# Two edits to a one-core transformer-block kernel: the first weight matrix is split before the first input is normalised, and the end of the last stage is rearranged

## The chip, the core and the metric

The kernel runs on one core of one Trainium2 chip, as one program. The metric is the device time of a run in microseconds, from start to end; the median of several runs is compared. A core has five engines that run their own instruction streams and wait for each other by semaphores: TensorE (PE, matmuls; its weight loads are shown as PEld), VectorE (DVE), ScalarE (ACT), GpSimd (POOL) and SyncE (SP), which here only issues the DMAs.

## The reference, cut to what matters

```python
xn = layernorm(x)                                   # x: 8 x 1024 rows of 512, no gain or offset
h  = performer_attn(xn, wq, wk, wv, wo, omega)      # random-feature attention, 16 heads
y  = layernorm(xn + h, ln1_g, ln1_b)
h2 = gelu(y @ w1 + b1) @ w2 + b2                    # 512 -> 2048 -> 512
a  = layernorm(y + h2, ln2_g, ln2_b)
r  = sigmoid(mix_r(xn) @ W_r.T) * (square(relu(mix_k(xn) @ W_k.T)) @ W_v.T)
return x + a + r
```

All is float32. Each product is made of three fast products: a matrix is split into a rounded part "hi" and a rest "lo", and hi*hi, hi*lo and lo*hi are summed (`TERMS`, `product`).

## The kernel before, in words

Three passes run one after the other: `keys_pass` (normalise x, queries, keys, values, the sums over keys), `attend_pass` (attention output and gated block) and `feed_forward_pass`. Each works on 32 groups of `GT` = 256 rows (tokens), a group being `TG` = 2 token tiles of 128 partitions. Each engine has its own program; the order of the jobs in it is written out by hand (`HEAD` and the `..._BODY` lists in the first pass, `BODY` in the last). An engine does its jobs strictly in that order, and a job begins with its semaphore waits.

**Start of the first pass.** SP issues the loads of omega, of the first group of x (`keys_xin`) and of six half matrices of weights (`keys_e` holds those of wk and wq, `keys_z_sum` those of wv, 512 KB each). For the first group: DVE makes the statistics (`stats`, L222 to L228), POOL inverts the deviation (`norm.invert`, L233 `rstd` and L235 `shift`), ACT normalises (`norm`, L475, `keys_xn`), PE transposes in two halves (`turn_x`, L608), ACT and DVE split each half into `xT_hi` (L482) and `xT_lo` (L546), and POOL adds the two for a copy to memory (`whole`, L442, `keys_xT_whole`). A weight matrix is split in two pieces: ACT rounds each into hi (L183), DVE takes the rest into lo (L190). PE's first product (job `k`) waits for the split xT and for both pieces of wk.

**The last pass.** Per group g, PE makes eight blocks of the hidden layer (`w1`, into `ffn_hidden`), each followed three steps later by its part of the second product (`w2`, into `ffn_result`): w1 0, 1, 2, w2 0, w1 3, w2 1, w1 4, w2 2, w1 5, w2 3, ... w1 7, the transposes of the next group's y (`turn`, L1514), w2 5, 6, 7. Between them ACT takes the gelu (L1451) and the rounded part (L1460), and DVE the rest `ffn_hT_lo` (L1484); w2 n waits for `hT_lo` n. In DVE's order the job `base` stands between `hT_lo` 2 and `hT_lo` 3: it waits for the DMA of `ffn_r_in` and makes `x_in` = 0.5 r + x (L1489). The end of a group: DVE adds `ffn_result` and `yb` into `ffn_s` (L1496) and makes the statistics; POOL inverts; ACT normalises `ffn_s` (L1464, two tiles); POOL multiplies by the gain (L1418), adds the offset (L1421) and adds `x_in` (L1425), each over both tiles at once; SP stores `x_in`. Then POOL makes `yb` of the next group (L1413). SP, after `yb`, loads the next y, waits for the store of `x_in` to have landed, and loads the next `x_in` and `r_in` (L1393, L1394). So `base` of a group waits for POOL's end of the group before. Groups 1 to 30 run in a hardware loop; groups 0 and 31 are written out.

Of the kernel before, what the change touches and what calls it, by code (L numbers as in the profile page):

```python
# [6 lines left out]
ALU = mybir.AluOpType  # L7
# [3 lines left out]
P = 128  # L11
D = 512
# [8 lines left out]
TG = 2  # L21
# [221 lines left out]
def keys_pass(nc, x, wq, wk, wv, omega, xn_d, xT_d, u_d, kv_d, n_batches, groups_per_batch):  # L243
# [5 lines left out]
    G = n_batches * groups_per_batch  # L249
# [5 lines left out]
    with ctx:  # L255
# [31 lines left out]
        norm = Norm(mem, ctx, "n0", EPS0)  # L287
# [55 lines left out]
        def rows(j):  # L343
# [15 lines left out]
        POOL_BODY = [("whole", 0, 1), ("z", 0, 0), ("stats", 0, 2), ("z", 1, 0), ("z", 2, 0), ("z", 3, 0),  # L359
                     ("z", 4, 0), ("z", 5, 0), ("z", 6, 0), ("z", 7, 0)]  # L360
        SP_BODY = [("x", 0, 2), ("whole", 0, 1), ("sums", 0, -1), ("q", 1, 1), ("norm", 0, 2)]
        HEAD = [("x", 0, 0), ("stats", 0, 0), ("norm", 0, 0), ("turn_x", 0, 0), ("turn_x", 1, 0), ("x", 0, 1),
                ("whole", 0, 0), ("weights", 0, 0), ("weights", 1, 0), ("k", 0, 0), ("weights", 2, 0), ("k", 1, 0),
                ("stats", 0, 1), ("sq", 0, 0), ("q", 0, 0), ("norm", 0, 1), ("sq", 1, 0), ("q", 1, 0),
                ("turn_k", 0, 0), ("turn_k", 1, 0), ("v", 0, 0), ("v_out", 0, 0), ("v", 1, 0), ("v_out", 1, 0),
                ("turn_x", 0, 1), ("turn_x", 1, 1)]
# [913 lines left out]
def feed_forward_pass(nc, x, w1, b1, w2, b2, ln2_g, ln2_b, y_d, r_d, out, n_groups):  # L1280

    G = n_groups
# [6 lines left out]
    with ctx:  # L1289
# [13 lines left out]
        s = sb("s", [P, TG, D])  # L1303
# [65 lines left out]
        def _(sp):  # L1369
            sp.dma_start(y[:, :, :], y_g[0]).then_inc(y_loaded, 16)  # L1370

            def do(job, n, g):
# [10 lines left out]
                if job == "base":  # L1383
# [8 lines left out]
                        sp.wait_ge(w_split, len(pieces))  # L1392
                    sp.dma_start(x_in[:, :, :], x_g[g]).then_inc(xr_loaded, 16)  # L1393
                    sp.dma_start(r_in[:, :, :], r_g[g]).then_inc(xr_loaded, 16)  # L1394
                if job == "end":
                    sp.wait_ge(done, g + 1)
                    sp.dma_start(out_g[g], x_in[:, :, :]).then_inc(stored, 16)

            run(sp, do)
            sp.wait_ge(y_loaded, 16 * (G + 1))  # L1400
            sp.wait_ge(stored, 16 * G)

        @block.gpsimd
        def _(pool):
            make_identity(pool, ident, ident_made)
            norm.init(pool)
            pool.wait_ge(consts_loaded, 16 * 4)

            def do(job, n, g):
                if job == "base":  # L1410
                    pool.wait_ge(y_loaded, 16 * g + 16)
                    wait(pool, sum_ready, TG * g)
                    pool.tensor_tensor(yb[:, :, :], y[:, :, :], bias2[:, :].unsqueeze(1).broadcast_to([P, TG, D]),  # L1413
                                       ALU.add).then_inc(yb_ready, 1)
                if job == "end":
                    norm.invert(pool, g)
                    pool.wait_ge(normed, TG * g + TG)
                    pool.tensor_tensor(s[:, :, :], s[:, :, :], gain[:, :].unsqueeze(1).broadcast_to([P, TG, D]),  # L1418
                                       ALU.mult).then_inc(gained, 1)
                    pool.wait_ge(gained, g + 1)  # L1420
                    pool.tensor_tensor(s[:, :, :], s[:, :, :], offset[:, :].unsqueeze(1).broadcast_to([P, TG, D]),  # L1421
                                       ALU.add).then_inc(offsets, 1)
                    pool.wait_ge(offsets, g + 1)
                    pool.wait_ge(base_ready, g + 1)
                    pool.tensor_tensor(x_in[:, :, :], s[:, :, :], x_in[:, :, :], ALU.add).then_inc(done, 1)  # L1425

            run(pool, do)
# [42 lines left out]
        def _(dve):  # L1470
            def do(job, n, g):
# [19 lines left out]
                if job == "end":  # L1491
                    for t in range(TG):
                        dve.wait_ge(result[t].full, g + 1)
                        dve.wait_ge(yb_ready, g + 1)
                        wait(dve, done, g)
                        dve.tensor_tensor(s[:, t, :], result[t].t[:, :], yb[:, t, :], ALU.add).then_inc(sum_ready, 1)  # L1496
                    dve.wait_ge(sum_ready, TG * g + TG)
                    wait(dve, norm.ready, g)
                    norm.reduce(dve, g, [s[:, t, :] for t in range(TG)])

            run(dve, do)

# [95 lines left out]
```

## Time and profile before

| | |
|---|---|
| median of 3 runs | 3691.76 us (3691.68 to 3693.3) |
| the profiled execution | 3692.05 us, its span 3690.2 us |
| PE, PEld, DVE, ACT, POOL busy | 96%, 84%, 56%, 50%, 38% |
| start of the last pass's steady part (first transposes) | 2228.48 us |

The span is what the profile covers; 1.85 us of the time lie outside it. Busy shares are means over the three passes and hide short waits, of which the start and the end of the program are made.

### The profile page before, as it was taken

How to read it: one execution, taken by the hardware profiler on the slowest of the kernel's cores; microseconds unless marked ns; L12 is line 12 of the kernel's file. 1: busy time of each engine (PE TensorE's matmuls, PEld its weight loads, DVE VectorE, ACT ScalarE, POOL GpSimd, SP SyncE). 2: the span in 40 equal slices, each digit the busy share in tenths (PEclk: the TensorE clock that was granted, in tenths of full speed). 3: DMA queues.
4: the chain of work that ended last, by engine and by line, in shares of the span. 5: the costliest groups of instructions: out<-in, count | busy, mean ns of one | idle time of the engine just before them, and what ended most of it. 6: DMA issues, size and time to landing. Idle time of an engine off the chain costs nothing. (4 is left out here: it accounts for less than half of the span.)

```text
span 3690.2 us, 71667 instructions
## 1 busy us (share of the span) xinstructions
PE 3544.2 (96%) x27762; PEld 3105.4 (84%) x27762; DVE 2070.7 (56%) x3304; ACT 1839.5 (50%) x3976; POOL 1394.2 (38%) x957
## 2 busy tenths in 40 slices
PE   7999999999699999999999949999999999999998
PEld 6888888887588888888888849988889989888887
DVE  5877777777567777777777633333333333333332
ACT  5777777777456656565665633333333323333332
POOL 2554545454244545454454412222222222222222
PEclk9999999999799999999999979999999999999999
DMA  2222222221223232232323241111111111111111
GB/s 104 87 78 70 90 78 73 73 88 54 95 81 102 82 97 91 88 97 88 102 84 98 83 129 68 46 44 43 45 44 46 45 38 46 44 43 45 45 45 46
DMA packets 151680, 262.70 MB, mean 71 GB/s; under 512 B 23184, under 2 KB 44176, under 8 KB 151440
## 3 DMA queue, kind: packets, MB, share of 16 engines
q1 hardware_dynamic: 151440, 259.46, 20.9%
q8 instruction: 155, 2.54, 0.3%
q14 instruction: 85, 0.70, 0.1%
HBM read 155.48 MB, written 103.94 MB: 70 GB/s over the span
## 5 line engine op out<-in xcount | busy, mean ns | idle before, releaser
L1484 DVE TENSOR_TENSOR ffn_hT_lo<-ffn_hid,ffn_hT_hi 128x512 fp32r<-128x512 f32 x256 | 334.3, 1334 | 489.4 <-ACT ffn_hT_hi L1460 489.4
L97 PE MATMUL ffn_hidden<-ffn_yT_hi,ffn_wa_hi 128*128 128x256 f32 x2048 | 573.3, 280 | 11.8 <-DVE ffn_yT_lo L1480 11.8
L97 PE MATMUL ffn_hidden<-ffn_yT_hi,ffn_wa_lo 128*128 128x256 f32 x2048 | 573.3, 280 | 0.0
L97 PE MATMUL ffn_hidden<-ffn_yT_lo,ffn_wa_hi 128*128 128x256 f32 x2048 | 572.3, 279 | 0.0
L1451 ACT ACTIVATE ffn_hid<-ffn_hidden,ffn_bias 128x256 f32<-128x256 f32 x512 | 213.2, 467 | 669.6 <-PE ffn_hidden L97 650.8
L233 POOL TENSOR_TENSOR ffn_n_rstd<-ffn_n_base,ffn_n_power 128x2 f32<-128x2 f32 x32 | 22.4, 700 | 1073.7 <-DVE ffn_n_negmean L228 1073.7
L97 PE MATMUL ffn_result<-ffn_wb_hi,ffn_hT_hi 128*128 128x512 f32 x1024 | 412.2, 403 | 2.6 <-DVE ffn_hT_lo L1484 2.6
L97 PE MATMUL ffn_result<-ffn_wb_hi,ffn_hT_lo 128*128 128x512 f32 x1024 | 404.5, 395 | 0.0
L97 PE MATMUL ffn_result<-ffn_wb_lo,ffn_hT_hi 128*128 128x512 f32 x1024 | 404.2, 395 | 0.0
L97 PEld LDWEIGHTS ffn_hidden<-ffn_yT_hi,ffn_wa_hi 128*128 128x128 f32 x2048 | 384.5, 188 | 20.8 <-DVE ffn_yT_lo L1480 12.1
L97 PEld LDWEIGHTS ffn_hidden<-ffn_yT_lo,ffn_wa_hi 128*128 128x128 f32 x2048 | 385.0, 188 | 8.8
L97 PEld LDWEIGHTS ffn_hidden<-ffn_yT_hi,ffn_wa_lo 128*128 128x128 f32 x2048 | 385.2, 188 | 0.0
L457 POOL TENSOR_TENSOR keys_z_sum<-keys_z_sum,keys_e 128x512 f32<-128x512 f32 x192 | 265.2, 1402 | 307.3 <-ACT keys_e L512 307.3
L512 ACT ACTIVATE keys_e<-keys_feat,keys_below 128x128 f32<-128x128 f32 x1024 | 280.6, 420 | 22.8 <-DVE keys_below L569 22.7
L575 DVE SCALAR_TENSOR_TENSOR keys_pk_lo<-keys_e,keys_pk_hi 128x512 fp32r<-128x512 f32 x256 | 219.3, 887 | 25.7 <-ACT keys_pk_hi L519 25.5
L97 PEld LDWEIGHTS ffn_result<-ffn_wb_hi,ffn_hT_hi 128*128 128x128 f32 x1024 | 192.1, 188 | 48.4 <-DVE ffn_hT_lo L1484 10.2
L97 PEld LDWEIGHTS ffn_result<-ffn_wb_hi,ffn_hT_lo 128*128 128x128 f32 x1024 | 192.2, 188 | 46.9
L1107 DVE TENSOR_REDUCE attend_top<-attend_feat 128x4 f32<-128x512 f32 x256 | 159.0, 684 | 125.3 <-PE attend_feat L1200 125.3
L1126 DVE SCALAR_TENSOR_TENSOR attend_pT_lo<-attend_feat,attend_pT_hi 128x512 fp32r<-128x512 f32 x256 | 163.3, 683 | 116.7 <-ACT attend_pT_hi L988 116.3
L97 PEld LDWEIGHTS ffn_result<-ffn_wb_lo,ffn_hT_hi 128*128 128x128 f32 x1024 | 192.4, 188 | 38.0
L565 DVE TENSOR_REDUCE keys_top<-keys_feat 128x4 f32<-128x512 f32 x256 | 159.0, 684 | 107.7 <-PE keys_feat L652 107.7
L1464 ACT ACTIVATE ffn_s<-ffn_s,ffn_n_shift,ffn_n_rstd 128x512 f32<-128x512 f32 x64 | 48.7, 809 | 338.7 <-POOL ffn_n_shift L235 338.7
(238 smaller groups left out, 9876.8 us busy)
## 6 DMA issues: line engine op xcount, KB each, us to landing
attend_uq<-u_d SPq DMA_DIRECT2D x33, 512.0 KB, 4.6
ffn_y_in<-y_d SPq DMA_DIRECT2D x33, 512.0 KB, 3.6
keys_xin<-in_L_attn_x_dram SPq DMA_DIRECT2D x32, 512.0 KB, 5.3
xn_d<-keys_xn SPq DMA_DIRECT2D x32, 512.0 KB, 4.2
xT_d<-keys_xT_whole SPq DMA_DIRECT2D x32, 512.0 KB, 2.6
u_d<-keys_uq SPq DMA_DIRECT2D x32, 512.0 KB, 2.8
attend_xTf<-xT_d SPq DMA_DIRECT2D x32, 512.0 KB, 5.1
r_d<-attend_gate SPq DMA_DIRECT2D x32, 512.0 KB, 3.2
```

What stands on the lines that cost most here:

```text
L97: last = pe.matmul(out, stationary[a], moving[b], start=start and n == 0, stop=stop and n == len(TERMS) - 1)
L233: pool.tensor_tensor(self.rstd[:, :], self.base[:, :], self.power[:, :], ALU.pow).then_inc(self.root, 1)
L457: pool.tensor_tensor((z_all if last_of_batch else z_sum)[:, c, :], z_sum[:, c, :], e[t][:, c, :], ALU.add).then_inc(z_added[t], 1)
L512: last = act.activation(e[t][:, c, j * M:(j + 1) * M], feat[j].t[:, c * M:(c + 1) * M], ACT.Exp, bias=below[:, t, h:h + 1])
L565: dve.tensor_reduce(top[:, n, :, j:j + 1], feat[j].t[:, :].rearrange("p (c m) -> p c m", c=NC), AX.X, ALU.max).then_inc(top_ready, 1)
L575: dve.scalar_tensor_tensor(out=pk[t].lo[:, c, :], in0=e[t][:, c, :], scalar=FLOOR, in1=f32(pk[t].hi[:, c, :]), op0=ALU.add, op1=ALU.subtract)\
L1107: dve.tensor_reduce(top[:, n, :, j:j + 1], feat[j].t[:, :].rearrange("p (c m) -> p c m", c=NC), AX.X, ALU.max).then_inc(feat[j].free, 1)
L1126: dve.scalar_tensor_tensor(out=pT[j].lo[:, :], in0=feat[j].t[:, :], scalar=FLOOR, in1=f32(pT[j].hi[:, :]), op0=ALU.add, op1=ALU.subtract)\
L1451: last = act.activation(hid[n % 2][:, a, :], bank.t[:, a * GT:(a + 1) * GT], ACT.Gelu, bias=bias1[:, 2 * n + a:2 * n + a + 1])
L1464: act.activation(s[:, t, :], s[:, t, :], ACT.Identity, bias=norm.shift[:, t:t + 1], scale=norm.rstd[:, t:t + 1]).then_inc(normed, 1)
L1484: dve.tensor_tensor(hT[n % HB].lo[:, :, :], hid[n % 2][:, :, :], f32(hT[n % HB].hi[:, :, :]), ALU.subtract).then_inc(h_ready[n % HB], 1)
```

## The change

Three edits. In `HEAD`, the job `("weights", 0, 0)` moves from behind the first group's normalisation and transposes to a place between its statistics and its normalisation. In the last pass, POOL adds the offset to `x_in` right after `base`, before the inversion, in every group, and no longer to `s` behind the gain. In the last group alone, POOL's multiplication and final addition go to DVE, by token tiles of 512 columns, and SP stores each tile by itself.

```diff
-        HEAD = [("x", 0, 0), ("stats", 0, 0), ("norm", 0, 0), ("turn_x", 0, 0), ("turn_x", 1, 0), ("x", 0, 1),
-                ("whole", 0, 0), ("weights", 0, 0), ("weights", 1, 0), ("k", 0, 0), ("weights", 2, 0), ("k", 1, 0),
+        HEAD = [("x", 0, 0), ("stats", 0, 0), ("weights", 0, 0), ("norm", 0, 0), ("turn_x", 0, 0), ("turn_x", 1, 0),
+                ("x", 0, 1), ("whole", 0, 0), ("weights", 1, 0), ("k", 0, 0), ("weights", 2, 0), ("k", 1, 0),
...
# SP
-                if job == "end":
+                if job == "end" and isinstance(g, int) and g == G - 1:
+                    for t in range(TG):
+                        sp.wait_ge(done, g + 1 + t)
+                        sp.dma_start(out_g[g][:, t, :], x_in[:, t, :]).then_inc(stored, 16)
+                elif job == "end":
                     sp.wait_ge(done, g + 1)
                     sp.dma_start(out_g[g], x_in[:, :, :]).then_inc(stored, 16)
...
# POOL
                 if job == "end":
+                    pool.wait_ge(base_ready, g + 1)
+                    pool.tensor_tensor(x_in[:, :, :], x_in[:, :, :], offset[:, :].unsqueeze(1).broadcast_to([P, TG, D]),
+                                       ALU.add).then_inc(offsets, 1)
                     norm.invert(pool, g)
+                if job == "end" and not (isinstance(g, int) and g == G - 1):
                     pool.wait_ge(normed, TG * g + TG)
                     pool.tensor_tensor(s[:, :, :], s[:, :, :], gain[:, :].unsqueeze(1).broadcast_to([P, TG, D]),
                                        ALU.mult).then_inc(gained, 1)
                     pool.wait_ge(gained, g + 1)
-                    pool.tensor_tensor(s[:, :, :], s[:, :, :], offset[:, :].unsqueeze(1).broadcast_to([P, TG, D]),
-                                       ALU.add).then_inc(offsets, 1)
                     pool.wait_ge(offsets, g + 1)
-                    pool.wait_ge(base_ready, g + 1)
                     pool.tensor_tensor(x_in[:, :, :], s[:, :, :], x_in[:, :, :], ALU.add).then_inc(done, 1)
...
# DVE
+                if job == "end" and isinstance(g, int) and g == G - 1:
+                    dve.wait_ge(offsets, G)
+                    for t in range(TG):
+                        dve.wait_ge(normed, TG * g + t + 1)
+                        dve.tensor_tensor(s[:, t, :], s[:, t, :], gain[:, :], ALU.mult).then_inc(gained, 1)
+                        dve.wait_ge(gained, g + 1 + t)
+                        dve.tensor_tensor(x_in[:, t, :], s[:, t, :], x_in[:, t, :], ALU.add).then_inc(done, 1)
```

What stands in a row on an engine, at the places the prediction speaks of. First VectorE at the start of the first pass (`keys_wk_lo` is the rest of the first weight matrix, `keys_xT_lo` that of the transposed first group); ScalarE's order changes alike, with `keys_wk_hi` now ahead of `keys_xn`:

```order
 L228 TENSOR_SCALAR keys_n_negmean<-keys_n_mv 128x2
+L190 TENSOR_TENSOR keys_wk_lo<-keys_e,keys_wk_hi 128x1024 x2
 L546 TENSOR_TENSOR keys_xT_lo<-keys_turn,keys_xT_hi 128x512 x2
-L190 TENSOR_TENSOR keys_wk_lo<-keys_e,keys_wk_hi 128x1024 x2
 L190 TENSOR_TENSOR keys_wq_lo<-keys_e,keys_wq_hi 128x1024 x2
```

The two instructions move from behind the split of xT to before it. Next GpSimd in the body of the last pass's loop:

```order
-L1413 TENSOR_TENSOR ffn_yb<-ffn_y_in,ffn_bias 128x1024
+L1417 TENSOR_TENSOR ffn_yb<-ffn_y_in,ffn_bias 128x1024
+L1420 REGISTER_ALU
+L1421 TENSOR_TENSOR ffn_x_in<-ffn_x_in,ffn_offset 128x1024
 L231 ISA
-L232 REGISTER_ALU
 L233 TENSOR_TENSOR ffn_n_rstd<-ffn_n_base,ffn_n_power 128x2
 L234 REGISTER_ALU
 L235 TENSOR_TENSOR ffn_n_shift<-ffn_n_negmean,ffn_n_rstd 128x2
-L1417 REGISTER_ALU
-L1418 TENSOR_TENSOR ffn_s<-ffn_s,ffn_gain 128x1024
-L1421 TENSOR_TENSOR ffn_s<-ffn_s,ffn_offset 128x1024
-L1425 TENSOR_TENSOR ffn_x_in<-ffn_s,ffn_x_in 128x1024
```

The addition of the offset goes from between gain and final addition to a place ahead of the inversion; gain and final addition follow the inversion as before, as L1426 and L1430. Last, the end of VectorE's program after the change:

```order
L1501 TENSOR_TENSOR ffn_s<-ffn_result,ffn_yb 128x512 x2
L222 BN_STATS ffn_n_stats<-ffn_s 128x6 x2
L225 BN_AGGR ffn_n_mv<-ffn_n_stats 128x2 x2
L227 TENSOR_SCALAR ffn_n_base<-ffn_n_mv 128x2
L228 TENSOR_SCALAR ffn_n_negmean<-ffn_n_mv 128x2
L1509 TENSOR_TENSOR ffn_s<-ffn_s,ffn_gain 128x512
L1511 TENSOR_TENSOR ffn_x_in<-ffn_s,ffn_x_in 128x512
L1509 TENSOR_TENSOR ffn_s<-ffn_s,ffn_gain 128x512
L1511 TENSOR_TENSOR ffn_x_in<-ffn_s,ffn_x_in 128x512
```

The last four rows are new; the two operations of 1024 columns that they replace have left GpSimd's program.

## Rows read from the trace of the kernel before

**Rows 1.** The page: the chain that ended last, by line

```profile
PE ffn_result L97 19%; PE ffn_hidden L97 18%; PE ffn_turn L1514 1%; DMA ffn_r_in<-r_d 1%; POOL ffn_s L1421 0%; POOL ffn_s L1418 0%; POOL ffn_yb L1413 0%; SPq L1376 0%; DMA ffn_s<-in_L_attn_w_dram 0%; ACT ffn_s L1464 0%; DVE ffn_s L1496 0%; POOL ffn_n_rstd L233 0%; DVE ffn_hT_lo L1484 0%; POOLq L1289 0%; SPq L1388 0%
```

**Rows 2.** Timeline of the first 22 us: start, duration, operation, [idle before, releaser]

```profile
9.32 0.20 POOL L235 TENSOR_TENSOR keys_n_shift<-keys_n_negmean,keys_n_rstd 128x2 f32<-128x2 f32 x1
9.55 1.52 ACT L475 ACTIVATE keys_xn<-keys_xin,keys_n_shift,keys_n_rstd 128x512 f32<-128x512 f32 x2 [4.87 <-POOL keys_n_shift L235]
...
15.41 1.99 ACT L183 ACTIVATE keys_wk_hi<-keys_e 128x1024 fp32r<-128x1024 f32 x2
15.55 0.69 DVE L546 TENSOR_TENSOR keys_xT_lo<-keys_turn,keys_xT_hi 128x512 fp32r<-128x512 f32 x1 [1.90 <-ACT keys_xT_hi L482]
16.32 2.35 POOL L442 TENSOR_TENSOR keys_xT_whole<-keys_xT_hi,keys_xT_lo 128x1024 f32<-128x1024 f32 x1 [6.81 <-DVE keys_xT_lo L546]
16.50 4.40 DVE L190 TENSOR_TENSOR keys_wk_lo<-keys_e,keys_wk_hi 128x1024 fp32r<-128x1024 f32 x2 [0.25 <-ACT keys_wk_hi L183]
...
20.95 0.80 PE L97 MATMUL keys_ring<-keys_wk_hi,keys_xT_hi 128*128 128x512 f32 x1 [6.06 <-DVE keys_wk_lo L190]
```

**Rows 3.** The instructions on `keys_wk_lo`: duration ns min/median/max, first and last start

```profile
L190 DVE TENSOR_TENSOR keys_wk_lo<-keys_e,keys_wk_hi x2: 1210/2238/3265, 16.5 to 19.7; 128x1024 fp32r<-128x1024 f32 x2
```

**Rows 4.** Loads of wk: issues, then landing after issue, first half and second half

```profile
3.08 0.98 SPq L161 DMA_DIRECT2D keys_e<-in_L_attn_wk_dram  x2
...
keys_e<-in_L_attn_wk_dram SPq DMA_DIRECT2D x1, 512.0 KB, 4.6
...
keys_e<-in_L_attn_wk_dram SPq DMA_DIRECT2D x1, 512.0 KB, 5.4
```

**Rows 5.** Stretches: length, busy (count) of PE, PEld, DVE, ACT, POOL, PEclk, DMA share, GB/s

```profile
20.90:25.80 4.90, 4.85 (x11) 3.84 (x12) 2.26 (x2) 0.00 (x0) 0.00 (x0) 1.00 0.00 0
25.80:34.30 8.50, 8.50 (x38) 6.99 (x37) 5.24 (x10) 5.21 (x8) 0.90 (x2) 1.00 0.00 0
```

**Rows 6.** Timeline of PE, last pass: transposes that open groups' periods, first, two neighbours, last

```profile
2228.48 0.38 PE L1514 MATMUL ffn_turn<-ffn_ident,ffn_y_in 128*128 128x128 f32 x2
...
3479.45 0.38 PE L1514 MATMUL ffn_turn<-ffn_ident,ffn_y_in 128*128 128x128 f32 x2
...
3525.57 0.38 PE L1514 MATMUL ffn_turn<-ffn_ident,ffn_y_in 128*128 128x128 f32 x2
...
3618.50 0.27 PE L1514 MATMUL ffn_turn<-ffn_ident,ffn_y_in 128*128 128x128 f32 x1
```

**Rows 7.** Waits in the last pass, 2200 to 3690 us: total, times, longest

```profile
PEld ffn_result L97 <- DVE ffn_hT_lo L1484: 10.2, 43, 1.7
```

**Rows 8.** Timeline of one group's end and the next group's `base`, by engine

```profile
3589.32 2.72 POOL L1421 TENSOR_TENSOR ffn_s<-ffn_s,ffn_offset 128x1024 f32<-128x1024 f32 x1
3594.82 2.85 POOL L1413 TENSOR_TENSOR ffn_yb<-ffn_y_in,ffn_bias 128x1024 f32<-128x1024 f32 x1
...
3605.26 1.23 DVE L1489 SCALAR_TENSOR_TENSOR ffn_x_in<-ffn_r_in,ffn_x_in 128x1024 f32<-128x1024 f32 x1 [9.85 <-DMA ffn_r_in<-r_d]
3606.40 1.28 DVE L1484 TENSOR_TENSOR ffn_hT_lo<-ffn_hid,ffn_hT_hi 128x512 fp32r<-128x512 f32 x2
...
3607.14 0.50 PE L97 MATMUL ffn_result<-ffn_wb_hi,ffn_hT_hi 128*128 128x512 f32 x1 [0.15 <-DVE ffn_hT_lo L1484]
```

**Rows 9.** Timeline of the last 20 us

```profile
3666.35 0.69 DVE L1484 TENSOR_TENSOR ffn_hT_lo<-ffn_hid,ffn_hT_hi 128x512 fp32r<-128x512 f32 x1 [4.93 <-ACT ffn_hT_hi L1460]
...
3676.91 1.52 ACT L1464 ACTIVATE ffn_s<-ffn_s,ffn_n_shift,ffn_n_rstd 128x512 f32<-128x512 f32 x2 [10.60 <-POOL ffn_n_shift L235]
3678.51 2.34 POOL L1418 TENSOR_TENSOR ffn_s<-ffn_s,ffn_gain 128x1024 f32<-128x1024 f32 x1 [1.63 <-ACT ffn_s L1464]
...
3685.70 0.39 SPq L1397 DMA_DIRECT2D out_dram<-ffn_x_in  x1
```

**Rows 10.** DMA from 3685 to 3691 us: busy tenths in 40 slices of 0.15 us, and landing

```profile
DMA  0000000000299999989800000000000001000000
...
out_dram<-ffn_x_in SPq DMA_DIRECT2D x1, 512.0 KB, 2.8
```

More of the change, by code:

```diff
@@ L1400, in _ @@
             sp.wait_ge(y_loaded, 16 * (G + 1))
-            sp.wait_ge(stored, 16 * G)
+            sp.wait_ge(stored, 16 * G + 16)
         @block.gpsimd
```

## The prediction

> **What bounds the kernel now.** The chain that ended last comes first [rows 1]: it lies almost wholly on TensorE, but a DMA of `ffn_r_in`, three GpSimd lines of the last pass and a few other waits stand in it. So a change off TensorE counts only where TensorE waits: at the start, at such a wait in the last pass, and at the end. The next views were read for these places.
>
> At the start the timeline shows TensorE's first product at 20.95 us, 0.05 after the second `keys_wk_lo` is done (16.50 + 4.40 = 20.90). The split of the input, its other condition, was complete at 15.55 + 0.69 = 16.24 [rows 2]. The first weight matrix is what is late there, by 4.66 us. It is late for two reasons: ScalarE rounds it only after the input's transposes, and its first rest took 3265 ns where the second took 1210 [rows 3], since GpSimd's `keys_xT_whole` ran from 16.32 to 18.67 [rows 2].
>
> In the last pass, the steps from transposes to transposes: 30 periods take 3618.50 - 2228.48 = 1390.0 us, 46.33 on average, where two neighbours are 3525.57 - 3479.45 = 46.12 apart, the least of the 30 [rows 6]. The surplus is 1390.0 - 30 x 46.12 = 6.4 us. Where it sits is seen in one period [rows 8]: `base` waits for `r_in` until 3605.26, `hT_lo` 3 stands behind it and ends at about 3606.40 + 0.65 = 3607.05, and TensorE starts w2 3 at 3607.14, after a wait of 0.15 and with a first matmul of 0.50. Waits for `hT_lo` come 43 times, 10.2 us in all, the longest 1.7 [rows 7]; part of them stand before w2 0, which waits behind ScalarE's end of the group, not behind `base`.
>
> At the end nothing runs beside the chain: ScalarE 1.52 us, three GpSimd operations from 3678.51, the store at 3685.70, and its landing after 2.8 us [rows 9, 10].
>
> **The change, part by part.** All sums are against the profiled execution, 3692.05 us (span 3690.2 and 1.85 outside it); the median of the runs is 0.29 lower.
>
> *First matrix ahead of the normalisation.* Eight instructions change place (two ACT, two DVE ahead of two `xn`, two `xT_hi`, two `xT_lo`); none is added and SP's queue keeps its order. The halves of wk land at 3.08 + 4.6 = 7.68 and about 3.57 + 5.4 = 8.97 [rows 4]. ScalarE takes about 1.04 each (1.99 for two [rows 2]), so it is done with both at about 10.0 and normalises then instead of at 9.55: 0.45 later. DVE's rests follow from about 8.75. Here something new can be late: `shift` on GpSimd at 9.32 reads two SBUF operands for 0.20 us, and would find the first rest, 1.21 us long [rows 3], under way. One such pair is seen [rows 2, 3]: the rest began behind `xT_whole` and lasted 18.67 - 16.50 + 1.1 = 3.27. If `shift` waits in the same way, until about 10.35, ScalarE starts at about 10.55, 1.0 later than now. I take 1.0; the other bound is 0.45. The split of the input is then complete at 17.24 and TensorE starts at 17.3, with both rests of wk done by about 12. Gain 3.65 us (4.2 by the other bound).
> Every product after it follows, if wq is ready: ScalarE rounds wq from about 16.4, GpSimd's `xT_whole` (2.35) holds DVE until 19.7, two rests of 1.21 end at about 22.1. TensorE asks for it 24 matmuls after 17.3. At the last pass's rate (46.12 us for 192 matmuls of 256 columns and 96 of 512, so 0.24 per 512) this is 23.1. So it is covered by 1 us even if TensorE is fast at once.
> TensorE's granted clock is 1.00 in both stretches, but 11 matmuls take 4.85 us after its 6 us of idleness, 0.44 each (the level of 1.2 GHz), and then 38 take 8.50, 0.22 each (2.4 GHz) [rows 5]. The slow stretch can come out shorter or longer behind a shorter pause: none at all would give 2.4 us more, all 24 matmuls of job `k` slow would cost 13 x 0.22 = 2.9. I take it as unchanged.
>
> The Trainium skill (SBUF — State Buffer, SBUF: two separate sides) says that a VectorE operation with two SBUF inputs and a GpSimd operation that reads SBUF exclude each other, the first to start keeping the ports for its whole length; by it `shift` waits and the sum is the 3.65 taken.
>
> *Offset on `x_in` after `base`, groups 0 to 30.* One operation of 1024 columns (2.72 [rows 8]) leaves the path from ScalarE's end to `done`, `yb`, the loads and `base`; it is not shortened but moved to a stretch in which GpSimd has nothing else to do. All four steps behind it (store, y load, `x_in`, `r_in`) start 2.72 earlier, so `hT_lo` 3 does too. The longest wait is 1.7 [rows 7], so all of the surplus goes: 6.4 us. What is moved lands right behind `base`, which ends at 3606.49 (old clock), while `hT_lo` 3 starts at 3606.40 [rows 8], before GpSimd can have its semaphore. So it runs first. `hT_lo` 4 is then held by up to 2.35, to 3607.68 + 2.35 - 2.72 = 3607.3, while TensorE asks for it only after w2 3 and w1 6, over 5 us after 3607. That cover gone, each us would cost 31. If instead `hT_lo` 3 is held, it ends at 3606.49 - 2.72 + 2.35 + 0.65 = 3606.8 instead of 3607.05, and nearly nothing is gained: bounds 6.4 and 0. I take 6.4, since the start at 3606.40 is the nearer row.
> In the last group the same operation lies a period after 3606.49, before 3656, 20 us before it is needed.
>
> *The last end on DVE, by tiles.* Removed: three GpSimd operations, 3678.51 to 3685.7. Added: four DVE operations of 512 columns with two SBUF inputs, like `hT_lo`, 0.69 [rows 9]. The first tile is normalised at 3676.91 + 0.76 = 3677.67, the second at 3678.43, before DVE asks for it. 3677.70 + 4 x 0.69 + 3 x 0.03 for the waits = 3680.55. The last store is issued at 3680.57 instead of 3685.70: 5.1 us (4.8 if each wait takes 0.1 more). It moves half as much. The data of the 512 KB flow in ten slices of 0.15 us, 1.5 us, from 0.8 after the issue [rows 10]; the first tile's store, issued 1.4 earlier, is out of the way. So half the data saves 0.75 (bounds 0 and 0.75; I take 0.75, since nothing else is in flight). Together 5.85.
>
> The Trainium skill (DMA: Bandwidth & Descriptors, Anatomy of one DMA — SWDGE (gpsimd) path) gives each DMA a fixed 2.0 us plus bytes at 436 GB/s, which speaks against cutting a store: by it the last half takes 2.6 us, 0.2 less than the whole here, and the sum falls by 0.55. It is written for DMAs of the GpSimd queue; the 512 KB would take 3.2 by it, and the row has 2.8, so the row is followed.
>
> Sum: 3.65 + 6.4 + 5.85 = 15.9; 3692.05 - 15.9 - 0.29 = 3675.9, rounded to 3676.
>
> **The rivals.** What a measurement of this kernel can tell from no change is 0.2%, 7.4 us.
> *GpSimd's offset holds `hT_lo` 3.* For it: the pairs of [rows 2, 3] show how fully one engine holds the other. Against it: the order of starts. Loop 0 to 3 instead of 6.4: 3679 to 3682.5.
> *The start gives little.* `shift` waits longer than thought, or the slow stretch of TensorE grows by its bound of 2.9: start 0.7, in all 3679.
> *It does not do what it says.* `r_in` lands no earlier, because the store or a load takes the 2.72 back, and the start gives nothing: only the end's 5.85 is left, 3686, no change that can be told. The loads follow GpSimd closely in the trace, which speaks against it.
> *Slower.* The place is DVE behind `base`. If `hT_lo` 3 is held by GpSimd for 2.35 while `r_in` comes no earlier, w2 3 stalls 2.35 in 31 groups, 73 us, less 9.5 from both ends: 3755. It decides from the point where `hT_lo` 3 ends 0.3 us later than today (31 x 0.3 = 9.5). With the lead of 2.72 it would end 0.25 earlier even when held.
>
> By the Trainium skill's page on SBUF (same section) the first to start keeps the ports, which speaks for `hT_lo` 3 running first, and against the first rival.
>
> **How the numbers follow.** The forecast 0.65 (its own range 3673.5 to 3678.5, from 2.4 of clock and 0.55 of port below, and the small terms above), GpSimd holding `hT_lo` 3 0.15, little at the start 0.08, no lead 0.08, slower 0.04. Below 3684.4 (faster by over 0.2%) lie the first three: 0.88. Within 0.2%: 0.09. Slower by over 0.2%: 0.03, since part of the last case stays small. The range 3672.5 to 3682.5 takes the first three in and leaves less than 2 in 10 out.
>
> **What would show it.** Start: first product at about 17.3; 20.3 or later makes the step wrong; `keys_xn` at 10.55 or 10.0 tells whether `shift` waited. Last pass: 30 periods of 46.12 in 1383.6 us, `base` 2.7 earlier in the period, no wait of w2 3; a second rest lengthened to about 3 us behind `base`, not the first. End: last store issued 3.7 us after ScalarE's start of the last normalisation, now 8.79, and landed in about 2.05. Wrong would be periods over 46.3, or a stall of w2 3.

## The result and the profile after

| | before | after |
|---|---|---|
| median | 3691.68 us (3685.24 to 3693.3, 5 runs) | 3670.18 us (3667.66 to 3673.67, 5 runs) |
| profiled execution, its span | 3692.05, 3690.2 | 3670.18, 3668.4 |

The ratio of the medians is 0.9948, 95% interval 0.9933 to 0.9962: 21.5 us less, where 15.9 were forecast. The time lies 2.3 us below the range of 3672.5 to 3682.5. The medians of the kernel before in the comparisons below (3688.6 to 3691.8) are its times beside the kernel in question. One of `head_only`'s 12 executions took 3920.77 us at a mean granted clock of 0.84, where its other executions show 0.983 or more; it is counted nowhere.

**Start.** The timeline of the first 22 us of the kernel after, to be laid beside [rows 2]:

```profile
7.71 1.06 ACT L183 ACTIVATE keys_wk_hi<-keys_e 128x1024 fp32r<-128x1024 f32 x1 [2.76 <-DMA keys_e<-in_L_attn_wk_dram]
...
8.80 1.23 DVE L190 TENSOR_TENSOR keys_wk_lo<-keys_e,keys_wk_hi 128x1024 fp32r<-128x1024 f32 x1 [0.44 <-ACT keys_wk_hi L183]
9.28 0.80 POOL L235 TENSOR_TENSOR keys_n_shift<-keys_n_negmean,keys_n_rstd 128x2 f32<-128x2 f32 x1
9.78 1.06 ACT L183 ACTIVATE keys_wk_hi<-keys_e 128x1024 fp32r<-128x1024 f32 x1 [1.02 <-DMA keys_e<-in_L_attn_wk_dram]
10.74 1.50 ACT L475 ACTIVATE keys_xn<-keys_xin,keys_n_shift,keys_n_rstd 128x512 f32<-128x512 f32 x2
...
16.74 0.69 DVE L546 TENSOR_TENSOR keys_xT_lo<-keys_turn,keys_xT_hi 128x512 fp32r<-128x512 f32 x1 [1.90 <-ACT keys_xT_hi L482]
...
17.58 0.76 PE L97 MATMUL keys_ring<-keys_wk_hi,keys_xT_hi 128*128 128x512 f32 x1 [1.50 <-DVE keys_xT_lo L546]
```

The first product starts at 17.58 instead of 20.95, and what releases it is now the split of x. `shift` took 0.80 instead of 0.20: it started at 9.28 under the first rest of wk and was over at 10.08, with the end of that rest (8.80 + 1.23 = 10.03). `keys_xn` started at 10.74, behind ScalarE's second rounding and not behind `shift`: the second half of wk landed late and put that rounding at 9.78.

**Last pass.** The view of the waits of the whole pass, beside [rows 7], has no line any more in which TensorE waits for `hT_lo`. It lists waits above 0.15 us; a shorter one is left, as shown below. One period, to be laid beside [rows 8] (this group's period opened at 3556.29), first GpSimd's timeline:

```profile
3568.46 0.70 POOL L233 TENSOR_TENSOR ffn_n_rstd<-ffn_n_base,ffn_n_power 128x2 f32<-128x2 f32 x1 [23.78 <-DVE ffn_n_negmean L228]
...
3573.55 2.73 POOL L1430 TENSOR_TENSOR ffn_x_in<-ffn_s,ffn_x_in 128x1024 f32<-128x1024 f32 x1
3576.25 2.85 POOL L1417 TENSOR_TENSOR ffn_yb<-ffn_y_in,ffn_bias 128x1024 f32<-128x1024 f32 x1
3587.25 2.78 POOL L1421 TENSOR_TENSOR ffn_x_in<-ffn_x_in,ffn_offset 128x1024 f32<-128x1024 f32 x1 [8.15 <-DVE ffn_x_in L1494]
```

And VectorE's in the same period:

```profile
3568.22 0.16 DVE L228 TENSOR_SCALAR ffn_n_negmean<-ffn_n_mv 128x2 f32<-128x2 f32 x1
3572.40 7.25 DVE L1489 TENSOR_TENSOR ffn_hT_lo<-ffn_hid,ffn_hT_hi 128x512 fp32r<-128x512 f32 x3 [4.03 <-ACT ffn_hT_hi L1465]
3585.95 1.22 DVE L1494 SCALAR_TENSOR_TENSOR ffn_x_in<-ffn_r_in,ffn_x_in 128x1024 f32<-128x1024 f32 x1 [6.30 <-DMA ffn_r_in<-r_d]
3587.09 3.49 DVE L1489 TENSOR_TENSOR ffn_hT_lo<-ffn_hid,ffn_hT_hi 128x512 fp32r<-128x512 f32 x2
```

The addition of the offset stands behind `base`, and two `hT_lo` beside it take 3.49, where two alone take 1.28 [rows 8]. `hT_lo` 3 started at 3587.09, before GpSimd's 3587.25, so the second one, `hT_lo` 4, was held. Nobody waits for it. The periods of TensorE, by the transposes that open them, the first and the last:

```profile
2221.30 0.60 PE L1526 MATMUL ffn_turn<-ffn_ident,ffn_y_in 128*128 128x128 f32 x4
...
3602.32 0.93 PE L1526 MATMUL ffn_turn<-ffn_ident,ffn_y_in 128*128 128x128 f32 x7
```

Thirty periods take 1381.02 us, 46.03 each, where they took 1390.0 [rows 6].

**End.** The timeline of the last 8 us, beside [rows 9, 10]:

```profile
3660.65 1.52 ACT L1469 ACTIVATE ffn_s<-ffn_s,ffn_n_shift,ffn_n_rstd 128x512 f32<-128x512 f32 x2 [10.60 <-POOL ffn_n_shift L235]
...
3661.57 0.69 DVE L1509 TENSOR_TENSOR ffn_s<-ffn_s,ffn_gain 128x512 f32<-128x512 f32 x1 [2.01 <-ACT ffn_s L1469]
3662.30 0.69 DVE L1511 TENSOR_TENSOR ffn_x_in<-ffn_s,ffn_x_in 128x512 f32<-128x512 f32 x1
3662.91 0.69 DVE L1509 TENSOR_TENSOR ffn_s<-ffn_s,ffn_gain 128x512 f32<-128x512 f32 x1
3663.02 1.69 SPq L1398 DMA_DIRECT2D out_dram<-ffn_x_in  x2
3663.63 0.69 DVE L1511 TENSOR_TENSOR ffn_x_in<-ffn_s,ffn_x_in 128x512 f32<-128x512 f32 x1
```

The DMA from 3663.4 to 3669, busy tenths in 40 slices of 0.14 us, and the landing:

```profile
DMA  0004998940001899881000000000000000200000
...
out_dram<-ffn_x_in SPq DMA_DIRECT2D x1, 256.0 KB, 2.1
```

The second addition ends 3.67 us after ScalarE's start; in the kernel before, the store was issued 8.79 us after it. The two stores flow one behind the other with a gap (the two humps), and the second lands after 2.1.

**Where the 21.8 us of the span went.** The first product 3.37 earlier; 3.81 more between it and the opening of the last pass's steady part (2228.48 to 2221.30 is 7.18); 9.00 in the 30 periods (1390.02 to 1381.02); and 5.6 from the last transposes to the span's end (3690.2 - 3618.50 = 71.70, and 3668.4 - 3602.32 = 66.08). Forecast were 3.65, nothing, 6.4 and 5.85. What has to be explained is 2.6 in the loop and 3.8 in stretches that the edits don't touch.

### The profile page after: what moved, and what is told of

Read it like the earlier page. It is cut to its first block and busy times, and to the rows that moved or that the text cites. A ratio compares the mean times of both kernels' runs of the same rounds, so it can differ in the third digit from the quotient of the medians.

```text
span 3668.4 us, 71700 instructions
## 1 busy us (share of the span) xinstructions
PE 3534.0 (96%) x27762; PEld 3100.5 (85%) x27762; DVE 2143.2 (58%) x3308; ACT 1839.6 (50%) x3976; POOL 1392.1 (38%) x955
## 5 line engine op out<-in xcount | busy, mean ns | idle before, releaser
L1489 DVE TENSOR_TENSOR ffn_hT_lo<-ffn_hid,ffn_hT_hi 128x512 fp32r<-128x512 f32 x256 | 403.0, 1603 | 500.9 <-ACT ffn_hT_hi L1465 500.9
L97 PE MATMUL ffn_hidden<-ffn_yT_hi,ffn_wa_hi 128*128 128x256 f32 x2048 | 573.8, 280 | 12.1 <-DVE ffn_yT_lo L1485 12.1
```

Of the source, the lines that this page charges most:

```text
L97: last = pe.matmul(out, stationary[a], moving[b], start=start and n == 0, stop=stop and n == len(TERMS) - 1)
L1489: dve.tensor_tensor(hT[n % HB].lo[:, :, :], hid[n % 2][:, :, :], f32(hT[n % HB].hi[:, :, :]), ALU.subtract).then_inc(h_ready[n % HB], 1)
```

## The experiments

**The kernel before again** (no edit), and each edit alone. `head_only` is the edit of `HEAD`; `end_only` the last group with its early offset, VectorE's tiles and two stores; `loop_only` is this, in all 32 groups:

```diff
 # POOL, job "end"
+                    pool.wait_ge(base_ready, g + 1)
+                    pool.tensor_tensor(x_in[:, :, :], x_in[:, :, :], offset[...], ALU.add).then_inc(offsets, 1)
                     norm.invert(pool, g)
...
-                    pool.tensor_tensor(s[:, :, :], s[:, :, :], offset[...], ALU.add).then_inc(offsets, 1)
-                    pool.wait_ge(base_ready, g + 1)
```

> The kernel before, unchanged, profiled a second time. In the first pair of profiles the changed kernel opened the last pass 7.2 us earlier (first transposes at 2221.3 against 2228.5), of which its first product at 17.58 instead of 20.95 explains 3.4. The other 3.8 lie in four places where TensorE ran at its slow cadence for longer in the one profile than in the other (4.7 against 1.7 us at about 48 us, 3.7 against 0 at 1015 to 1027, 5.6 against 2.6 at 2150, and 2.6 against 4.1 at 2190, the other way). Theory chance: where the slow stretches fall differs from one execution of the same kernel to the next, so this second profile opens the last pass anywhere from 2223 to 2231, with other lengths at these four places, and the five times spread over some 6 us. Theory systematic: they belong to the kernel; this profile repeats 2228.5 within 0.5 and the same four lengths. Both: the 30 periods of the last pass are 46.12 us at the least and sum to 1388 to 1392.

> Only the first matrix ahead of the normalisation. Both theories: first product at 17.6, last pass as before (periods 46.12 and more, about 1390 in all). Theory chance: median 3.4 us under the kernel before, within its spread of some 4 us, and the four slow places take any of their lengths. Theory systematic (the earlier start itself shortens later slow stretches): median 7 us under, first transposes of the last pass at 2221.3 within 0.5.

> Only the offset added to x_in right after base, in all groups; start and end as before, the last end on GpSimd with two operations instead of three. Last pass: 30 periods of 46.03, 1381.0 in all, 9.0 less than 1390.0 (6.4 from w2 3, 2.7 from w2 0). The last end is one GpSimd operation shorter, 2.4. Median 11.4 us under the kernel before. The forecast's own reckoning (46.12 per period, no gain before w2 0) would give 6.4 + 2.4 = 8.8. The rival that GpSimd holds hT_lo 3 would give 2.4 to 5.4; it is already unlikely, since the profile of the changed kernel has hT_lo 3 right behind base.

> Only the last group's end on DVE by token tiles with two stores; its offset is added early in this group alone, groups 0 to 30 as before. The last store issued 3.7 us after ScalarE's last normalisation starts instead of 8.8, landing in 2.1 instead of 2.8: 5.1 + 0.7 = 5.8 us by the forecast. In the profile of the changed kernel the span ends 2.0 us after that landing instead of 1.7, so 5.5. If a cut store cost a fixed 2 us, the landing would take 2.6 and the gain be 5.1. Periods as before.

| | median | beside before's | ratio, interval | first product | steady part opens | 30 periods |
|---|---|---|---|---|---|---|
| before again | 3691.18 | 3691.8 | 1.0 (0.9992 to 1.0009) | 20.91 | 2226.2 | 1393.3 |
| head only | 3687.92 | 3691.8 | 0.9991 (0.9983 to 1.0) | 17.04 | 2217.7 | 1392.4 |
| loop only | 3677.31 | 3691.8 | 0.996 (0.9947 to 0.9973) | 21.01 | 2225.2 | 1381.0 |
| end only | 3686.35 | 3691.8 | 0.9986 (0.9978 to 0.9995) | 20.85 | 2228.0 | 1393.4 |

The end alone is worth 5.4, as forecast (5.85), and the three parts add up: loop only gives 14.5, of which 2.4 lie behind the last transposes (69.36 to the end instead of 71.70) and are a part of the end's 5.4; 12.1 + 5.4 + 3.9 = 21.4 against 21.5 for all. So, by the medians, the surplus over the forecast is the loop's. Two things show in it. The old loop's 30 periods vary with the execution, and the profile that the forecast was made from (1390.0) is on the low side: the five others with the old loop gave 1393.3, 1392.4, 1393.4, 1395.2 and 1387.05. The new loop, where nothing else was done to it, gave 1381.0 in all nine, to within 0.1. And the period is 46.03, not the 46.12 that the forecast took as its floor.

**What lowered the floor.** In [rows 8]'s group, `rstd` started at 3584.22, 0.32 after the start of VectorE's last statistic; the timeline of before:

```profile
3583.90 0.16 DVE L228 TENSOR_SCALAR ffn_n_negmean<-ffn_n_mv 128x2 f32<-128x2 f32 x1
...
3584.22 0.70 POOL L233 TENSOR_TENSOR ffn_n_rstd<-ffn_n_base,ffn_n_power 128x2 f32<-128x2 f32 x1 [32.95 <-DVE ffn_n_negmean L228]
```

After, it is 3568.46 - 3568.22 = 0.24. The order of GpSimd's instructions, shown with the change, has the candidate: a REGISTER_ALU stood between `invert`'s instructions (L232), and stands ahead of them since (L1420), where the first wait for g + 1 now is. To tell it from the addition itself, only the wait is put ahead:

```diff
                 if job == "end":
+                    pool.wait_ge(base_ready, g + 1)
                     norm.invert(pool, g)
...
-                    pool.wait_ge(base_ready, g + 1)
                     pool.tensor_tensor(x_in[:, :, :], s[:, :, :], x_in[:, :, :], ALU.add).then_inc(done, 1)
```

> The kernel before with one edit: GpSimd's wait for base_ready (value g + 1) stands ahead of the inversion instead of ahead of the last addition. No operation moves; but the loop's register instruction that makes the value g + 1 then runs while GpSimd idles, and not between the end of DVE's statistics and rstd. Theory register: this is what shortens every period of the changed kernel by 0.09 us at w2 0; here too rstd starts 0.24 us after DVE's last statistics row starts instead of 0.32, and the least period is 46.03 instead of 46.12, with the surplus from w2 3 still there (30 periods sum to about 1389). Theory load (w2 0 comes earlier because GpSimd has one operation less at the group's end): least period stays 46.12.

Its timeline, the same two rows:

```profile
3580.41 0.16 DVE L228 TENSOR_SCALAR ffn_n_negmean<-ffn_n_mv 128x2 f32<-128x2 f32 x1
...
3580.65 0.70 POOL L233 TENSOR_TENSOR ffn_n_rstd<-ffn_n_base,ffn_n_power 128x2 f32<-128x2 f32 x1 [32.59 <-DVE ffn_n_negmean L228]
```

A single time of 3688.24 beside 3690.06. The distance is 0.24, and the least period is 46.03 with the offset where it was (the sum 1386.5, since `base` still stalls some). This edit moves the wait and the register instruction together. The kernel before tells them apart: in groups 0 and 31, which are written out and have the wait in its old place but no register instruction, the distance is 0.24 too, against 0.32 or 0.33 in the 30 groups of the loop, and the period behind group 0 is already 46.02 in end_only and 46.04 in before_third. So 30 x 0.09 = 2.7 us of the loop's gain is the register instruction's place: `rstd`, and with it ScalarE's end of the group and all that stands behind it up to `hT_lo` 0, comes that much earlier. `hT_lo` 0's wait went from 4.11 to 4.03.

The period of 46.03 isn't free of a wait either. TensorE's rows from the last matmul of w1 2 to the first of w2 0, first before:

```profile
3589.60 0.28 PE L97 MATMUL ffn_hidden<-ffn_yT_hi,ffn_wa_lo 128*128 128x256 f32 x1
3589.85 0.50 PE L97 MATMUL ffn_result<-ffn_wb_hi,ffn_hT_hi 128*128 128x512 f32 x1
```

Then after, with GpSimd's multiplication by the gain ahead of it, and last the same step into w2 1, for which nothing is late:

```profile
3571.07 2.41 POOL L1426 TENSOR_TENSOR ffn_s<-ffn_s,ffn_gain 128x1024 f32<-128x1024 f32 x1 [1.64 <-ACT ffn_s L1469]
...
3573.93 0.28 PE L97 MATMUL ffn_hidden<-ffn_yT_hi,ffn_wa_lo 128*128 128x256 f32 x1
3574.08 0.50 PE L97 MATMUL ffn_result<-ffn_wb_hi,ffn_hT_hi 128*128 128x512 f32 x1
3574.41 0.40 PE L97 MATMUL ffn_result<-ffn_wb_lo,ffn_hT_hi 128*128 128x512 f32 x1
...
3579.69 0.28 PE L97 MATMUL ffn_hidden<-ffn_yT_hi,ffn_wa_lo 128*128 128x256 f32 x1
3579.81 0.40 PE L97 MATMUL ffn_result<-ffn_wb_hi,ffn_hT_hi 128*128 128x512 f32 x1
3580.04 0.39 PE L97 MATMUL ffn_result<-ffn_wb_lo,ffn_hT_hi 128*128 128x512 f32 x1
```

From start to start the step into w2 0 takes 0.25 before, 0.15 after and 0.12 without a wait, and its first matmul another 0.10 more than w2 1's (0.33 against 0.23). So some 0.13 us a period, 4 us in 30, are still lost at w2 0 (an estimate from these rows). `hT_lo` 0 itself took 1.62 us (3572.40 to 3574.02) where 0.69 is its length alone: it started while that multiplication ran. No run tried to take this away.

**GpSimd's offset ahead of `hT_lo` 3.** The first rival's order, forced:

```diff
 # DVE
                 if job == "w1":
+                    if n == 3 and not (isinstance(g, int) and g == 0):
+                        dve.wait_ge(offsets, g + 1)
                     dve.wait_ge(h_hi[n % 2], (NH // 2) * g + n // 2 + 1)
```

> The changed kernel, but hT_lo 3 waits for the offset's addition on GpSimd in groups 1 to 31. This is the rival of the forecast, made to happen: hT_lo 3 ends about 2.8 us later than in the changed kernel, which is where it ended in the kernel before or 0.1 to 0.3 earlier. So the lead is just used up: periods 46.03 when r_in lands well, and a surplus like that of the kernel before (6 to 12 us in 30 periods, 1387 to 1393) otherwise. Median 3676 to 3682 against 3670 of the changed kernel. If the lead is more than the 2.7 us of one operation, the periods stay at 46.03 throughout (1381).

3672.56 (3671.7 to 3673.33), 0.9957 (0.9941 to 0.9972) beside 3690.06: milder than expected. `hT_lo` 3 waited 2.51 behind the addition (3588.97, 2.40 long), and the periods sum to 1383.4, 2.4 over the new floor. In the two groups shown, `base` came 29.66 us into the period after the change and 33.29 before it (3585.95 - 3556.29 against 3605.26 - 3571.97), 3.6 earlier, but 0.7 of that is one landing: `r_in` landed 5.3 us after its issue there and 6.0 before. Over all 31 groups `base` comes 2.9 earlier (30.06 against 32.99 on average), and the landings are alike, 5.7 on average in both profiles and from 5.1 to 7.4 in single groups. Held, `hT_lo` 3 ends 4.43 after `base`'s start (3591.40 + 0.69 - 3587.66), where it was 1.79 in [rows 8]: 30.08 + 4.43 = 34.51 us into the period on average against 32.99 + 1.79 = 34.78. So 0.3 us of lead is left. It counts for much, since only late landings stall w2 3. In the profile of before no group in which `r_in` landed within 5.75 us of its issue did; 14 of the 15 later ones did, by the time over 5.67 (0.12 at 5.79, 1.73 at 7.40). Held, the same edge lies at 5.87, and 4 groups are over it. The order was worth little here; a held `hT_lo` 3 would not have undone the gain.

**A rung more on GpSimd's path**, on the kernel before (the offset is added twice, so the output is not the reference's):

```diff
                     pool.tensor_tensor(s[:, :, :], s[:, :, :], offset[...], ALU.add).then_inc(offsets, 1)
-                    pool.wait_ge(offsets, g + 1)
+                    pool.wait_ge(offsets, 2 * g + 1)
+                    pool.tensor_tensor(s[:, :, :], s[:, :, :], offset[...], ALU.add).then_inc(offsets, 1)
+                    pool.wait_ge(offsets, 2 * g + 2)
```

> The kernel before with one more GpSimd operation of 1024 columns at the end of every group (the offset is added twice, so the output differs by it). The dose the other way: done, yb, the loads and base come 2.7 us later, and hT_lo 3, which is late by 0 to 1.7 already, is late by 2.8 to 4.5 in each of 31 groups. Periods 49 us, 30 of them 1470 to 1480; with the end's own operation (2.4) the median is 80 to 95 us above the kernel before. If the surplus did not come from this chain, the median rises by the end's 2.4 alone.

3784.6 (3781.14 to 3787.78), 1.026 (1.0244 to 1.0275): 94.5 us more, as expected, with periods of 49.19 on average. The same 2.73 us on the same path costs 95 when added, and gave about 8 when taken away (11 less the register instruction's 2.7): the path had hardly any slack, and on the other side TensorE's own work, with what is left of w2 0's wait, is the floor.

**One store at the end**, on the kernel after:

```diff
-                    for t in range(TG):
-                        sp.wait_ge(done, g + 1 + t)
-                        sp.dma_start(out_g[g][:, t, :], x_in[:, t, :]).then_inc(stored, 16)
+                    sp.wait_ge(done, g + 2)
+                    sp.dma_start(out_g[g], x_in[:, :, :]).then_inc(stored, 16)
...
-            sp.wait_ge(stored, 16 * G + 16)
+            sp.wait_ge(stored, 16 * G)
```

> The changed kernel with the last group stored by one DMA of 512 KB after both tiles, instead of one of 256 KB for each. The store is issued at the same time as the second one before (3.7 us after ScalarE's last normalisation starts); landing in 2.8 instead of 2.1 us, so the span from the last transposes is 0.7 us longer (66.8 instead of 66.1). If each DMA carried a fixed 2 us, so that the half store took 2.6, it would be 0.2.

The DMA from 3661 to 3667, 40 slices of 0.15 us, and the landing:

```profile
DMA  0000000000999999999100000000000000200000
...
out_dram<-ffn_x_in SPq DMA_DIRECT2D x1, 512.0 KB, 2.8
```

From the last transposes (3599.57) to the span's end it takes 66.83, against 66.08 with two stores and 66.01 in a second profile: the split is worth 0.75 to 0.8, as the forecast had it. Its single time, 3668.14 beside 3688.64, is below the others for another reason, which the next part gives.

**The start, split further.** The second half of wk is split behind `norm`, and VectorE's first rest waits until `shift` is done:

```diff
-            return range(n * n_w // 3, (n + 1) * n_w // 3)
+            return (range(0, 1), range(2, 4), range(4, 6), range(1, 2))[n]
...
-        HEAD = [("x", 0, 0), ("stats", 0, 0), ("weights", 0, 0), ("norm", 0, 0), ("turn_x", 0, 0), ("turn_x", 1, 0),
+        HEAD = [("x", 0, 0), ("stats", 0, 0), ("weights", 0, 0), ("norm", 0, 0), ("weights", 3, 0), ("turn_x", 0, 0),
...
 # DVE, job "weights"
+                    if n == 0:
+                        dve.wait_ge(norm.ready, 1)
```

> The changed kernel with a finer order at the start: ScalarE rounds the first half of wk, normalises, then rounds the second half while TensorE transposes; DVE's first rest waits until GpSimd's shift is done. shift is then held by nobody (0.20 instead of 0.80 us) and xn starts at 9.5 instead of 10.2 to 10.7; the second rest pushes the first xT_lo by about 0.3. First product at 16.5 instead of 17.0 to 17.6, so 0.6 to 1.1 us, too little for the medians to tell from the changed kernel (3668 to 3671). If the pair of rests in the gap costs more than the hold, the first product comes at 17.5 or later.

Its timeline at the start:

```profile
9.23 0.19 POOL L235 TENSOR_TENSOR keys_n_shift<-keys_n_negmean,keys_n_rstd 128x2 f32<-128x2 f32 x1
9.46 1.23 DVE L190 TENSOR_TENSOR keys_wk_lo<-keys_e,keys_wk_hi 128x1024 fp32r<-128x1024 f32 x1 [1.15 <-POOL keys_n_shift L235]
11.96 1.23 DVE L190 TENSOR_TENSOR keys_wk_lo<-keys_e,keys_wk_hi 128x1024 fp32r<-128x1024 f32 x1 [1.27 <-ACT keys_wk_hi L183]
```

`shift` takes 0.19 again, and the first product starts at 16.53. That is 0.5 to 1.0 earlier than in the kernel after, by its three profiles (17.58, 17.04, 17.08). The median does not show it: 3670.36 here and, again,

> The finer start once more. First product at 16.5. Median 0.5 to 1.1 us under after_third if only the first product counts, which these rounds can hardly tell; its profile adds one to the side of the new start. Its first profile opened the last pass at 2223.0, later than most with the new start, which the theory systematic would not have expected.

3670.04 (0.9943, 0.9929 to 0.9956), beside 3670.18, 3672.72 and 3668.22 for the kernel after. No kernel tried measurably beats the changed one.

**How much the start is worth, and where 3.8 us came from.** The kernel after with the old `HEAD`, and the kernel after again, side by side, twice; and head only and the kernel before again:

> The changed kernel with the start put back: offset after base and the last end on DVE, but wk split behind the transposes as in the kernel before. By the runs so far the last pass gives about 11.3 us on average (its 30 periods came out at 1390.0, 1393.3, 1392.4, 1393.4 in four profiles with the old loop and at 1381.0 in the new one) and the end 5.5: median 17 us under the kernel before, 3674 to 3675, and the start's share is what the changed kernel has beyond that. Theory direct: the start is worth its first product, 3.4 to 3.9 us, no more. Theory systematic: it also shortens later slow stretches, and is worth 6 to 7 us; rest_only is then at 3676 to 3677.

> The changed kernel again, on the chip of rest_only. First product at 17.0 or 17.6, according to when the second half of wk lands (9.06 in one profile, 9.78 in the other). Periods 46.03, 1381.0. Theory direct: 3.4 to 3.9 us under rest_only, first transposes of the last pass anywhere from 2217 to 2225. Theory systematic: 6 to 7 us under rest_only, and these transposes at 2218 to 2221.

> The changed kernel with the old start once more. 30 periods at 1381.0, from the last transposes to the end 66.0. Theory direct: 3.4 to 3.9 us above after_third in the median. Theory systematic: 5.5 to 6.5 us above it.

> The changed kernel once more, on the chip of rest_twice. First product at 17.0 or 17.6. Theory direct: median 3.4 to 3.9 us under rest_twice, first transposes of the last pass 3.4 to 3.9 earlier on average over all profiles. Theory systematic: 5.5 to 6.5 us under rest_twice, these transposes at 2219 to 2222.

> The kernel with the start alone once more, for its profile. Theory direct: where TensorE's slow stretches fall is chance, the first transposes of the last pass come anywhere between 2217 and 2225, the stretch at about 45 us lasts between 0 and 5. Theory systematic: 2217 to 2219 again, and no slow stretch above 2 us at about 45.

> The kernel before once more. First product at 20.9, first transposes of the last pass at 2223 to 2229, 30 periods 1387 to 1393.5. Theory direct: anywhere in this range. Theory systematic: 2226 or later.

Old `HEAD` 3673.58 and 3677.04, new `HEAD` 3672.72 and 3668.22: a start worth 0.9 in one pair, 8.8 in the other, 3.9 in head only; 4.5 on average. A single execution of head only again took 3680.24 beside 3688.64, 8.4 less; its 30 periods, 1387.05, and its clock (below) were both on the fast side. So the medians put the start's worth anywhere from 1 to 9 us; the openings below say more. The kernel before, a third time, was 1.0002 (0.9993 to 1.0011). What scatters them is seen in TensorE's stretches from 40 to 56 us and from 1008 to 1026 (length, PE busy and count, granted clock, DMA share, GB/s). They are cut at the same times, not at the same matmul, so the counts differ. First the kernel before:

```profile
40.00:56.00 16.00, 14.34 (x95) 0.79 0.13 51
1008.00:1026.00 18.00, 14.65 (x136) 0.81 0.33 105
```

The kernel after:

```profile
40.00:56.00 16.00, 14.34 (x144) 0.89 0.09 35
1008.00:1026.00 18.00, 14.70 (x180) 1.00 0.34 107
```

The old `HEAD` with the rest of the change (rest_twice):

```profile
40.00:56.00 16.00, 14.34 (x150) 1.00 0.09 35
1008.00:1026.00 18.00, 14.65 (x184) 1.00 0.33 108
```

And the kernel after again (after_again):

```profile
40.00:56.00 16.00, 14.97 (x136) 0.79 0.09 35
1008.00:1026.00 18.00, 15.39 (x170) 0.81 0.30 89
```

In the stretch from 40 us the clock is at its lower level (0.50) for some 7, 3.5 or 0 us of the 16, behind 4 us of which TensorE is busy 2.3. Finer stretches of the kernel before:

```profile
42.00:44.00 2.00, 1.53 (x9) 1.00 0.00 0
44.00:46.00 2.00, 0.80 (x12) 1.00 0.00 0
46.00:48.00 2.00, 2.00 (x49) 0.61 0.00 0
48.00:50.00 2.00, 2.00 (x5) 0.50 0.00 0
50.00:52.00 2.00, 2.00 (x6) 0.50 0.65 262
```

Over all 18 profiles, by the clock in the two stretches:

| clock at 40, at 1008 | old `HEAD`: opens at | new `HEAD`: opens at | apart, means | first product apart |
|---|---|---|---|---|
| 0.79, 0.81 | 2228.5, 2228.0, 2228.1, 2227.9, 2227.3 | 2223.85, 2223.0 | 4.5 | 4.1 |
| 0.89, 0.81 to 1.00 | 2226.2, 2225.2 | 2221.3, 2220.5, 2220.2 | 5.0 | 3.9 |
| 1.00, 0.91 to 1.00 | 2223.1, 2222.15 | 2219.6, 2218.6, 2218.95, 2217.7 | 3.9 | 3.7 |

At the same clock the opening moves by about what the first product moves (means of the same profiles; the two profiles of the finer start stand with the new `HEAD`). From the first product to the opening it is 2206.4 to 2207.5 us in the seven profiles of the first row, 2203.4 to 2205.3 in the five of the second and 2200.7 to 2202.1 in the six of the third, old and new `HEAD` mixed. From the first row to the last the clock moves it by about 5 us (5.3 with the old `HEAD`, 4.7 with the new), with no edit between. So the 3.8 us were, most of them, the clock of two executions: 0.79 and 0.81 in the one profiled of before, 0.89 and 1.00 in that of after. Whether the earlier start makes the higher clock likelier stays open: 0.79 came in 5 of 9 old and 2 of 9 new, 1.00 in 2 of 9 and 4 of 9, which so few can't tell from chance.

## Why the prediction was right, and where it was not

**The place of the gain: right.** All three parts showed where they were put, and the sum missed by 5.6 of 21.5 on the side of too little.

**The start: right in its terms, partly by luck.** First product forecast 17.3, measured 17.58, 17.04 and 17.08. `shift` was held until the rest ended, as taken, but was over at 10.08, not at 10.35: by the forecast's own rows it was 8.75 + 1.21 + 0.20 = 10.16, and nothing in them gives the rest of its 1.0. By the Trainium skill (SBUF — State Buffer, SBUF: two separate sides) the first to start holds the ports for its whole instruction; these rows agree, with `shift` at 0.80 beside the rest and 0.19 without it; `rstd`'s, in the last section, does not. `keys_xn` was forecast at 10.55 behind `shift`; it came at 10.74 behind the late landing of wk's second half, and at 10.20 and 10.25 in the two other profiles, right behind `shift` (over at 10.17 and 10.16) and the second rounding. "Every product after it follows, if wq is ready" held too: at like clocks the last pass opened 3.9 to 5.0 earlier.

**The step "I take it as unchanged" failed.** It looked at one slow stretch of TensorE, at the first product. That one was alike in the profiled pair (11 slow matmuls before [rows 5], 12 after), but over the 18 profiles it has 7 to 14 with the old `HEAD` and 6 to 12 with the new, and the 24 matmuls of job `k` start to start take 6.9 to 8.5 us. Others, which it did not look for, such as those at about 46 and 1015 us, differ between executions by several us. That belongs to the width of the range, more than to its middle: it is as large as the whole start.

**The loop's term, 6.4, was mis-sized; it measured 9.0 in the profiled pair and about 11 on average.** The mechanism was right (no wait of w2 3, `hT_lo` 3 first, `hT_lo` 4 held; "`base` 2.7 earlier" came out as 2.9 on average). The step that failed is "the surplus is 1390.0 - 30 x 46.12": the least of 30 periods was taken for a floor, but each of them held a delay of 0.09 at w2 0, which the changed order removed (wait_early: 46.03, 2.7 in all). The prediction saw that part of the 10.2 us of waits stands before w2 0, and put its change at nothing: it is half of them, 30 of the 43, at 0.17 each. The row that moved, L232's REGISTER_ALU, was in the order printed with the change, and got no price. In the profiled pair this is the whole miss of the term: 9.0 - 2.7 = 6.3, for 6.4. The other part is the sample: the 30 periods exceeded the new loop's 1381.0 by 9.0 in the profile used, and by 12.3, 11.4, 12.4, 14.2 and 6.0 in the five others.

**The end: right.** 5.85 forecast, 5.6 in the profiled pair, 5.4 (0.9986) alone. ScalarE's start to the second tile's end took 3.67 for 3.64. Of the landing, the row was followed and not the Trainium skill's fixed 2.0 us plus bytes (DMA: Bandwidth & Descriptors, Anatomy of one DMA — SWDGE (gpsimd) path). The rows agree with the choice for these stores of SP's queue: 2.1 for 256 KB and 2.8 for 512 KB, and cutting the store saved 0.75, where the page's 2.6 for the last half would have left 0.2 of it. But the page's own two estimates, 3.2 and 2.6, differ by 0.6, so it does not speak against cutting a store, as the prediction had it; they lie 0.4 and 0.5 above the measured ones.

**The rivals.** The first came out weaker than priced when forced (2.4 of stall, 3672.56, not 3679 to 3682.5). Its lead was sized about right (0.25, and 0.3 on average); what the prediction missed is that a few tenths spare most of a stall that only late landings cause. "It does not do what it says" and "slower" did not occur. That the path is as tight as the slower rival says is shown by one_more.

## What to carry to other kernels

The least period of a loop is a floor only if nothing in it waits: look into the least one too, at every wait, down to 0.1 us, and price a register instruction that the new order moves off a path like any other (0.09 us x 30). A surplus read from one profile is one draw: where it comes from waits near their edge (here landings of 5.1 to 7.4 us with the edge at 5.7), several profiles of the unchanged kernel say more than a closer reading of one. And a step on a path without slack costs its full length per group when it is added, but gives back only what TensorE waited when it is removed.

## What the runs showed of the hardware

- A register instruction between GpSimd's wait and its next operation costs 0.08 us (0.32 against 0.24 from VectorE's row to `rstd`, in wait_early and in the written-out groups of the kernel before).
- A 128x2 operation of GpSimd was held by a 128x1024 one of VectorE for its rest (0.80), yet `rstd`, the same size, did not lengthen the rest of 1.23 that began 0.31 after it (8.80 against 8.49). The other way round, a VectorE operation of 512 columns that started under a 1024-column multiplication of GpSimd took 1.62 instead of 0.69.
- The granted clock fell to 0.50 for 0, 3.5 or 7 us at the same place of the program from one execution to the next, while the 30 periods of the new loop agreed within 0.1 us in nine profiles.
